# Routing of a batch's tokens at 0.62, 0.69 and 0.84 of the next batch's turn

## The reference

```
x = x + self_attention(layernorm(x))                     # band of 64, softmax
q, k, v = norm @ W_Q.T, ctx @ W_K.T, ctx @ W_V.T         # 16 heads of 64, norm = layernorm(x)
x = x + softmax(where(mask, -10000, q k / 8)) v @ W_out.T + b_out
xf = layernorm(x)
logits = xf @ Wg                                         # 1600 tokens x 16 experts
topi = top_k(logits, 2); gates = softmax(logits on topi)
y = sum over e of (silu(xf W1[e] + b1[e]) * (xf W11[e] + b11[e]) @ W2[e] + b2[e]) * gates[:, e]
x = x + y + shared_expert(xf)
```

## Time and profile before

| | us |
|---|---|
| median of three runs | 1487.9 |
| lowest and highest | 1484.02, 1489.26 |
| the profiled execution, its own time | 1489.42 |
| the span of its trace | 1487.7 |
| PE, DVE, ACT, POOL busy | 1397.3, 1113.6, 876.4, 913.7 |

### The profile page before, as it was taken

The page is one execution under the profiler, slowest core; times in us unless marked ns, Lnnn a source line. Parts: engine busy times, 40 slices in busy tenths (PEclk is TensorE's granted clock), DMA queues, the critical chain, the costliest instruction groups (busy, mean ns, idle before and its releaser), DMA issues. The chain is left out here.

```text
span 1487.7 us, 29710 instructions
## 1 busy us (share of the span) xinstructions
PE 1397.3 (94%) x10219; PEld 1342.0 (90%) x10219; DVE 1113.6 (75%) x2883; ACT 876.4 (59%) x1659; POOL 913.7 (61%) x980
## 2 busy tenths in 40 slices
PE   7689999999999999999999999999999999977795
PEld 5589999999999999999999999999999999966585
DVE  5667787777777777877787877777877777759565
ACT  5556665656566656566666656565656565557353
POOL 2466566656666666666656676666666676536364
PEclk9889999999999999999999999999999999998898
DMA  4344352423323241414241514141413221116322
GB/s 125 73 113 114 81 144 56 118 65 96 93 68 117 63 138 49 135 48 122 55 133 44 150 46 122 45 117 46 117 51 96 56 81 52 37 45 177 85 64 92
DMA packets 164810, 131.20 MB, mean 88 GB/s; under 512 B 79189, under 2 KB 158822, under 8 KB 164150
## 3 DMA queue, kind: packets, MB, share of 16 engines
q1 hardware_dynamic: 160868, 123.63, 30.2%
q0 software_dynamic: 3360, 5.47, 1.1%
q10 hardware_dynamic: 434, 0.20, 0.0%
HBM read 96.08 MB, written 38.34 MB: 90 GB/s over the span
## 5 line engine op out<-in xcount | busy, mean ns | idle before, releaser
L1525 ACT CAST pT_hi<-banks 128x512 fp32r<-128x512 f32 (+1 forms) x672 | 357.2, 538 | 395.3 <-PE banks L1695 387.4
L1586 DVE TENSOR_TENSOR pT_lo<-banks,pT_hi 128x512 fp32r<-128x512 f32 (+1 forms) x576 | 354.8, 625 | 202.6 <-ACT pT_hi L1525 199.1
L1468 POOL TENSOR_SCALAR probs<-probs,row_inv 128x1408 f32<-128x1408 f32 x192 | 278.0, 1448 | 228.7 <-DVE row_inv L1639 227.2
L1461 POOL TENSOR_SCALAR bias<-mask,c_all 128x1444 f32<-128x1444 uint8 (+1 forms) x208 | 306.5, 1473 | 138.9 <-DVE nmax L1574 107.4
L1695 PE MATMUL banks<-ident,probs 128*128 128x128 f32 (+1 forms) x2304 | 366.0, 274 | 21.7 <-POOL probs_half L1470 11.2
L1727 PE MATMUL banks<-pT_hi,ctx_hi 128*128 128x256 f32 (+1 forms) x1056 | 326.4, 309 | 5.0 <-DVE ctxT_lo L1606 5.0
L1516 ACT ACTIVATE probs<-probs,nmax 128x1448 f32<-128x1448 f32 x192 | 289.6, 1508 | 56.4 <-DVE nmax L1574 54.5
L1695 PEld LDWEIGHTS banks<-ident,probs 128*128 128x128 f32 (+1 forms) x2304 | 268.8, 140 | 38.3 <-DVE pT_lo L1586 18.8
L1727 PE MATMUL banks<-pT_lo,ctx_hi 128*128 128x256 f32 (+1 forms) x1056 | 302.1, 286 | 0.0
L1727 PE MATMUL banks<-pT_hi,ctx_lo 128*128 128x256 f32 (+1 forms) x1056 | 301.8, 286 | 0.0
L1677 PE MATMUL banks<-ctxT_hi,qh 128*128 128x362 f32 (+1 forms) x832 | 240.0, 370 | 2.7 <-PEq L665 2.6
(11 more groups left out here) (334 smaller groups left out, 2071.5 us busy)
## 6 DMA issues: line engine op xcount, KB each, us to landing
mask<-mask_dram SPq DMA_DIRECT2D x192, 180.5 KB, 2.4
q_dram<-stage SPq DMA_DIRECT2D x96, 200.0 KB, 3.1
nat<-in_ctx SPq DMA_DIRECT2D x16, 704.0 KB
qh<-q_dram SPq DMA_DIRECT2D x14, 800.0 KB, 5.1
ql<-q_dram SPq DMA_DIRECT2D x14, 800.0 KB, 6.6
mask_dram<-in_mask_BxSxS_bk SPq DMA_DIRECT2D x32, 141.0 KB, 2.7
nat<-in_L_ffn_W SPq DMA_DIRECT2D x30, 128.0 KB
q_dram<-stage SPq DMA_DIRECT2D x32, 100.0 KB, 2.1
```

What stands on the lines that cost most here:

```text
L1461: pool.tensor_scalar(bias[(t + b) % 2][0:n, 0:SK], masks[s][0:n, :], MASKED, c_all[0:n, b, t:t + 1], ALU.mult, ALU.add).then_inc(bias_read ...
L1468: pool.tensor_scalar(prob(j)[0:n, 0:FIRST], prob(j)[0:n, 0:FIRST], rinv[0:n, s:s + 1], 1.0, ALU.mult, ALU.mult)
L1525: act.copy(pT_hi[tslot(b, j)][:, 0:w], banks[:, T_BANK + j % 2, 0:w]).then_inc(turned_hi, 1)
L1586: dve.tensor_tensor(p_lo, turn, p_hi.bitcast(F32), ALU.subtract).then_inc(turned_lo, 1)
```

## The change

Three places in `tensor_order` are different numbers, and the ranks of batch b-1 now stand in turn b, where they stood in turn b+1. Three latenesses of routing steps behind the projection are raised: VectorE's `shift`, ScalarE's `normalise` and GpSimd's `rstd`. All five queues are written from these numbers.

```
-        turn += [(at, kind, bb, 0) for at, kind, bb in ((0.875, "turn", b - 1), (0.93, "logits", b - 1),
-                                                        (0.055, "ranks", b - 2)) if bb < NB - 1]
+        turn += [(at, kind, bb, 0) for at, kind, bb in ((0.62, "turn", b - 1), (0.69, "logits", b - 1),
+                                                        (0.84, "ranks", b - 1)) if bb < NB - 1]
...
-    "project": ((2.2, "stats"), (3.2, "aggregate"), (4.2, "epsilon"), (9.2, "shift")),
+    "project": ((2.2, "stats"), (3.2, "aggregate"), (4.2, "epsilon"), (10.2, "shift")),
...
-            out.append((n + 12.0, "normalise", b, 0))
+            out.append((n + 12.6, "normalise", b, 0))
...
-            out.append((n + 6.0, "rstd", b, 0))
+            out.append((n + 8.0, "rstd", b, 0))
```

## The result

The changed kernel takes 1588.0 us (median of 4 runs, 1584.5 to 1591.1), the kernel before 1486.5 beside it: ratio 1.068, 95% interval 1.065 to 1.071. The profiled execution spans 1585.2 us. The forecast was 1585 us, and the two waits that it named are there.

The account below looks back on a forecast made before the run. TensorE, busy 94% of the span, was taken as the bound. Turns 1 to 13 at 1.8 + 3.5 + 1.7 + 0.7 - 1.1 = 6.6 give 86, turns 14 and 15 12, turn 16 -1: +97, 1585 us, range 1545 to 1620.

Parts of the forecast that it names:

- The wait for the logits: TensorE, first matmul of group 2: waits for VectorE's read of the logits (L490), 1.8 us a turn, bounds 1.2 to 1.9.
- The wait for the ranks: TensorE, first step of group 3: waits for VectorE's read of the ranks (L527), 3.5 us a turn, bounds 2.9 to 4.4.
- The chain: VectorE's total, inverse, second, less, expert, put between the last two scores ahead of the ranks: 1.34 us of that wait.
- The clock behind the ranks: TensorE work lost to a lowered clock after the ranks' wait: 1.7 us a turn.
- Behind the logits: TensorE work lost to a lowered clock after the logits' wait: 0.7 us a turn, four times in ten.
- Rival 1: The waits come but the clock stays: 4.2 us per turn, 1549 us; chance 0.18.
- rival 2: Both waits are followed by low clock, 3.4 us behind the ranks, 1.7 behind the logits: 1625 us; chance 0.11.
- What is won: Routing leaves the place before the half tile, so TensorE's old waits there go: 1.1 us a turn, or 0.
- the two old waits: TensorE's waits for the normalised half tile (9.4 us in 13 turns) and lower parts (4.8 us), forecast to go.
- Turn 16: It loses the routing of batch 14 and with it a TensorE wait of 1.15 us: -1.
- rival 3: SP: mask loads behind the wait for scattered rows come late, delaying GpSimd's bias: 21 us more, 1606 us; chance 0.08.
- The edits at no cost: Later reciprocal root (0.7 us to spare), ScalarE normalising, moved send and SP stores were claimed to cost nothing.

Follow-up runs that it names:

- e6: Changed kernel with VectorE's chain (total, inverse, second, less, expert) wholly ahead of the reciprocal L1639, at 9.2 to 9.5 behind the logits: 1579.4 us, ratio 1.061.
- e5: Changed kernel with VectorE's chain total to expert at 8.0 to 8.7 behind the logits instead of 9.2 to 9.9: 1557.7 us, ratio 1.047.
- e4: Changed kernel with 34 identity transposes added right behind the ranks, so TensorE works through most of the wait on L527: 1567.2 us, ratio 1.056.
- e2: Changed kernel with logits at 0.70 and ranks at 0.86, each moved behind the one step it stood ahead of: 1493.1 us, ratio 1.005.
- e3: Changed kernel with the ranks alone moved, from 0.84 to 0.92; logits stay right ahead of group 2: 1538.9 us, ratio 1.037.
- e7: Changed kernel with logits at 0.70 and ranks at 0.885, two steps behind the start of group 3: 1488.5 us, ratio 0.9996.
- e12: Kernel before with only the three latenesses altered (shift 10.2, normalise n + 12.6, rstd n + 8.0): 1486.5 us, ratio 0.9998.
- e8: e3 with 16 identity transposes added right behind the logits: 1540.8 us, ratio 1.035.

## Why the prediction was right, step by step

The two waits, their places and the clock behind them were right; that the sum met the time within 3 us is in part luck, since errors of some 9 us one way and 3 the other stand in it. Turns 1 to 13 lengthened by 6.8 us on average (77.7 to 84.5, from one logits matmul to the next); forecast 6.6. The terms:

- **The wait for the logits**, 1.8: measured 1.70 in all 15 turns. VectorE takes the score ahead first, as read from the earlier trace rows.
- **The wait for the ranks**, 3.5: measured 4.1 in turns 1 to 13 and 3.5 and 2.9 in the last two (2.9 each). Over 15 turns that is 60.1 us where 51.3 were forecast. This is the term that was mis-sized, in both of its parts. The chain was reckoned at 1.34 us with the earlier trace rows as the price, 0.66 at most for one of its operations; it takes 0.80 us in six of the 13 turns and 2.01 in the other seven, in which it meets the start of a normalisation and L521 is held up (e6). The rest was reckoned at 2.0 + 0.2; the wait less the chain is 2.6 to 2.8 us in 12 of the 13 turns, and why it is longer stays open. So the 3.3 to 3.7 us of e6, without GpSimd beside the chain, meet the forecast of 3.5 because the two errors cancel, and that e5 saves 1.34 us a turn, just what the chain was reckoned at, is chance too. L499, a cast of 200 values ahead of the chain, takes 1.39 us in the median, but in turns 9 to 11 VectorE stands idle 1.4 to 1.5 us between it and the chain, so it isn't what is missing there. The upper bound of 4.4 was broken in 7 of 13 turns.
- **The clock behind the ranks**, 1.7: 2.1 us behind each of 13 waits, nothing behind one of 2.91 us. **Behind the logits**, 0.7: 6.6 / 15 = 0.44. With the logits' wait the two come to 25.5 + 34.1 = 59.6 us, where 15 x (1.8 + 1.7 + 0.7) = 63 were forecast, and e4 shows that the clock's part is real. Rival 1 (the clock stays) and rival 2 (3.4 us each) are both out.
- **What is won**, 1.1 a turn: the two old waits did go in turns 1 to 15. For the half tile the rows show how. Its last score on TensorE and VectorE's part of the same score, turn 10 of the kernel before and then of the changed one:

```profile
922.26 0.50 PE L1677 MATMUL banks<-ctxT_hi,ql 128*64 128x362 f32 x2
924.07 0.96 DVE L1574 CUSTOM_DVE_ANT_0 probs_half<-banks,bias,nmax 64x724 f32<-64x724 f32 x1
...
987.56 0.49 PE L1677 MATMUL banks<-ctxT_hi,ql 128*64 128x362 f32 x2
988.50 0.95 DVE L1574 CUSTOM_DVE_ANT_0 probs_half<-banks,bias,nmax 64x724 f32<-64x724 f32 x1
```

  VectorE starts 1.31 us after TensorE has ended, and in the changed kernel 0.45; what follows, from there to the end of the normalisation, takes 6.6 us in the median of both. Two reasons for that are left, and no run separates them. One is the forecast's: before, routing (L499 to L507) stands right ahead of that score, in the changed kernel its last operation (L537) nearly 7 us ahead. The other is that TensorE has stood still for 5.8 us earlier in the turn, and VectorE caught up; then the gain is part of the loss. For the second speak turns 14 and 15 of e2: without that stand VectorE is 1.79 us behind, though the last routing operation starts 5.9 us ahead. For the first speaks turn 0 of the kernel before, a lighter turn without routing and without such a stand: VectorE is 0.47 us behind, and the wait is 0.03. So does e3, where TensorE stands 2.5 to 3.9 us in each of turns 1 to 13 and the half tile still waits 0.56 to 0.81, with an L537 that starts 1.0 us ahead. e7 decides nothing here, though it has no such stand and its half tile waits 0.82: its later ranks put an L537 of 1.26 us only 3.3 us ahead of the score.
- **Turn 16**, -1: the wait of 1.15 us is still there (row below), though TensorE had stood for the ranks of turn 15 as well. But the stretch ahead of it is shorter: from the end of the half tile's last score to this row it is 8.3 us in the kernel before and 6.8 in the changed one. VectorE took that score 0.42 us behind TensorE instead of 1.95. So what was forecast was won, only not at the wait that was named.

```profile
1410.76 0.44 PE L1695 MATMUL banks<-ident,probs 128*128 128x128 f32 x2 [1.14 <-POOL probs_half L1470]
```

- **SP**, rival 3: the loading of x1 waits 209 us instead of the 174 of the earlier trace rows, and GpSimd's waits for masks are 28.2 us in all; no wait of TensorE shows that goes back to them. **The edits at no cost** cost nothing (e12).

From the profiled terms: 60.1 + 25.5 + 34.1, less the 11.2 + 8.6 of the old waits but the 1.5 left, is 101; the spans differ by 97.5, and what makes up the 4 us between is open.

## What to carry to other kernels

An instruction that borrows a buffer has two ends to keep clear of: what must be read out before it may write, and who takes the buffer next. Count, in the order of the waiting engine, how much work lies on either side, and compare that with how far the reading engine lags; here the guests' waits of 1.7 and 4.1 us say that about as much work was missing between them and the next user, and one place in the order, for two guests, was worth 6% (e2). When a wait vanishes beside a new and larger one, don't book it as a gain at once: ask first whether the new wait is what hides it. Here that stayed open.

## What the hardware showed

A stall of TensorE has no fixed price in clock. Waits of 1.7 us lowered it 4 times in 15 in the changed kernel and in e6, 7 in 15 in e5, once in 15 in e3 and never in e4; waits of about 2 us once in 5 in e3 and 8 times in 10 in e8; the waits of 1.8 to 3.0 us for L527 in e5 7 times in 15; waits of 3.3 to 4.8 us each time in the changed kernel and e6, for 1.3 to 3.0 us of lost work each. Filling the stall with idle matmuls gave all of it back (e4), at the price of what the filling overran.
